# Block 0 of a fused eight-stage transformer kernel: the bf16 parts of the row maxima made on GpSimd, not on VectorE

## The chip, the cores and the metric

One core of a Trainium2 chip runs the whole program. The metric is the device time in microseconds of one execution, as the median of several runs. One execution is profiled, and its trace gives the start and duration of every instruction on every engine.

## The reference

The input is x of 16 batches x 56 tokens x 128 features, a conditioning vector per batch, and a context of 16 x 1500 x 128. Eight stages follow, each adding its result to x: four attention stages and four feed-forward ones. The change lies in the first, six layers of adaptive layer norm, self-attention with rotary embedding, cross-attention to the context and an MLP. Its attention is the usual one, with 16 heads of 8 features:

```python
def _attn(q, k, v, mask):
    scores = jnp.einsum('bqhd,bkhd->bhqk', q, k) / np.float32(np.sqrt(HD))
    scores = jnp.where(mask[:, None, None, :], jnp.float32(-jnp.inf), scores)
    w = jax.nn.softmax(scores, axis=-1)
    return jnp.einsum('bhqk,bkhd->bqhd', w, v)
```

In the cross-attention each of 16 batches has 56 queries and 1500 keys per head; over six layers these are 96 passes.

## The kernel before

The kernel computes the softmax's exponentials with keys on the partitions and queries along the columns, so the row maximum of a query can't be taken there. It is taken beforehand from a second set of score products with queries on the partitions, and is then fed into the first set of products as extra rows of the matmul: the maxima, negated, are split into three bf16 parts (high, middle, low) whose sum has nearly float32 precision, and the key side has rows of ones for them.

A pass is called a batch here, numbered 0 to 95 (16 a layer). Block 0 runs over slots s, each of 12 steps kt = 0 to 11. Every engine's program walks the same slots and steps in the order written in the code, and semaphores connect them. In slot s:

- `score_tensor` (L1528) makes the scores of batch s, a step's 125 keys at a time in two halves, ScalarE takes their exponentials (L2019), and `weigh_tensor` (L1554) multiplies them with the values one step later.
- `max_tensor` (L1542) makes the second set of products, two a step. Their maxima are taken on VectorE (L1898) out of two PSUM banks that alternate, into `row_max`, 112 queries x 8 head pairs x 3 thirds of the keys. Steps 0 to 9 finish batch s + 1, steps 10 and 11 begin batch s + 2.
- The keys of batches s + 2 and s + 3 are projected (L1568), rotated and split into bf16 parts by VectorE (L1778, L1779), GpSimd (L2039 to L2049) and ScalarE (L1924, L1928), and the sync engine's queue moves the parts into `key_stack` (L1443), the mask rows (L1451) and the query parts into `query_stack` (L1461). The values are projected by L1576.
- At step 10 VectorE makes the parts of batch s + 1 (`max_parts_vector`, L1742 to L1750): the minimum over the three thirds of the negated maxima, then four operations of 112 x 8 elements, each waiting for the one before. TensorE then turns them (L1605, the `("rows", s + 1)` entry). At step 11 VectorE copies the turned rows to the query stack (`rows_vector`, L1794), ahead of its two maxima of that step, and TensorE's first scores of batch s + 1 wait for that copy.

A phase is 8 slots. Beside the cross-attention of 8 batches it carries, for the other half of the tokens, the MLP, the norms (`norm_gpsimd`, L2073 to L2078, in two halves at two successive steps), the rotary projections (L1650) and the self-attention. In GpSimd's program a step runs `query_gpsimd`, `key_gpsimd`, the norm halves and then the block-diagonal queries (L2111).

Order of GpSimd's steps, as written:

```python
if 0 <= s + 2 < NS:
    self.query_gpsimd(e, s, kt)
self.key_gpsimd(e, s, kt)
```

Of the kernel before, what the change touches and what calls it, by code (L numbers as in the profile page):

```python
# [7 lines left out]
ALU, ACT, AX = mybir.AluOpType, mybir.ActivationFunctionType, mybir.AxisListType  # L8
# [18 lines left out]
PAIRS, F2 = H // 2, 2 * D // H  # L27
# [77 lines left out]
def of_batch(a, b):  # L105
    return a[:, b * S:(b + 1) * S]
# [6 lines left out]
def spread(cols, n):  # L113
    p, m = cols.shape
    return cols.unsqueeze(2).broadcast_to([p, m, n])
# [67 lines left out]
class Setup:  # L183
# [19 lines left out]
    def gpsimd(self, e):  # L203
        k = self.k
        e.memset(k.ident[:, :], 0.0)
        e.memset(k.eps_col, EPS)
        e.memset(k.mean_w, 1.0 / D)
        e.drain()
        e.affine_select(out=k.ident[:, :], in_=k.ident[:, :], compare_op=ALU.not_equal, fill=1.0,
                        base=0, pattern=[[-1, 128]], channel_multiplier=1)  # L210
        e.drain()
        e.tensor_copy(k.ident_b[:, :], k.ident[:, :])
        e.drain().then_inc(k.consts_ready.sem, 1)
        e.wait_ge(k.select_arrived.sem, k.select_arrived())
        e.tensor_copy(k.gate_select, k.gate_select32).then_inc(k.select_ready.sem, 1)
# [992 lines left out]
NS = NL * B  # L1208
# [20 lines left out]
class Block0:  # L1229
# [507 lines left out]

    def max_parts_vector(self, e, s):

        neg, m = self.neg, self.m_part[:, 1:1 + 3 * PAIRS].rearrange("q (p j) -> q p j", j=3)  # L1740
        e.wait_ge(self.max_read.sem, self.max_read(s, 3 * PAIRS - 1))
        e.tensor_reduce(neg, self.largest[:, :, :], AX.X, ALU.min).then_inc(self.negated.sem, 1)  # L1742
        e.wait_ge(self.negated.sem, self.negated(s, 0))
        e.tensor_copy(m[:, :, 0], neg).then_inc(self.negated.sem, 1)
        e.wait_ge(self.negated.sem, self.negated(s, 1))
        e.tensor_tensor(neg, neg, m[:, :, 0], ALU.subtract).then_inc(self.negated.sem, 1)
        e.wait_ge(self.negated.sem, self.negated(s, 2))
        e.tensor_copy(m[:, :, 1], neg).then_inc(self.negated.sem, 1)
        e.wait_ge(self.negated.sem, self.negated(s, 3))
        e.tensor_tensor(m[:, :, 2], neg, m[:, :, 1], ALU.subtract).then_inc(self.parts_ready.sem, 1)  # L1750
# [331 lines left out]
    def gpsimd(self, e):  # L2082
        side = self.side
        e.memset(self.src_mask, 0.0)
        e.drain()
        for ks in self.k_stack:
            e.memset(ks[ROWS:ROWS_ALL, :, :], 0.0)
        e.drain().then_inc(self.zeros_ready.sem, 1)
        for s in self.slots():
            for kt in range(KT):  # L2090
                if 12 * (s % BH) + kt == T_MASKS and s < 0:
                    e.wait_ge(self.tables_arrived.sem, self.tables_arrived())
                    e.tensor_scalar(self.src_mask[0:1, :], self.src_mask8, LOW, None, ALU.mult)
                    e.tensor_scalar(self.mask_rows, self.ctx_mask8, LOW, None, ALU.mult)
                    e.drain().then_inc(self.masks_ready.sem, 1)
                if 0 <= s + 2 < NS:
                    self.query_gpsimd(e, s, kt)
                self.key_gpsimd(e, s, kt)
                ph, t = s // BH, 12 * (s % BH) + kt
                for name, at in T_NORM.items():  # L2100
                    layer = MLP_OF(ph) if name == "mlp" else NEXT_OF(ph)
                    if layer is not None and t - at - 5 in range(2):
                        self.norm_gpsimd(e, name, ph, layer, t - at - 5)
                for i, a in enumerate(T_SELF(ph) if NEXT_OF(ph) is not None else ()):
                    if t == a - 1:
                        if i == 0:
                            e.wait_ge(self.roped.sem, self.roped(ph, 0))
                        if i >= 2:
                            e.wait_ge(side.filled, side.at("sc", ph, i - 2))
                        q = of_batch(self.q_rot, SIDE_OF(ph) * BH + i).unsqueeze(1).broadcast_to([128, H, S])  # L2110
                        e.tensor_tensor(self.qd[:, i % 2, :].rearrange("p (h q) -> p h q", h=H), q,  # L2111
                                        spread(self.block_diag, S), ALU.mult).then_inc(self.q_blocked.sem, 1)
# [1506 lines left out]
```

## Time and profile before

| | us |
|---|---|
| median of 3 runs | 6531.23 |
| lowest and highest run | 6515.23, 6531.41 |
| the profiled execution's time | 6515.7 |
| its span in the trace | 6513.8 |
| block 0's batches, from the first to the last making of parts | 187 to 3356 in the span |

A row of the timeline has the start in us from the span's start, the duration, the engine, the line of the kernel, the operation, the tiles written and read, their shapes and how many instructions are merged; in brackets stands the engine's idle time before it and who ended that. PE is TensorE, DVE VectorE, ACT ScalarE, POOL GpSimd and SPq the sync engine's queue of transfers.

### The profile page before, as it was taken

The numbers are of one execution on the slowest core, as the hardware profiler recorded it, in microseconds if no ns is written. First come the engines' busy times: TensorE is split into PE (matmuls) and PEld (weight loads), VectorE is DVE, ScalarE is ACT, GpSimd is POOL, SyncE is SP. The second block draws the span as 40 slices with busy tenths as digits, with TensorE's granted clock in tenths as the row PEclk, the third lists the DMA queues.
The fourth block names the chain that finished last, engine by engine and source line by source line (L and its number), as shares of the span: only waits on it lengthen the run. The fifth ranks groups of instructions, "written<-read, shape, count | busy, mean of one in ns | idle before, by whom it ended". The sixth has DMA issues, their size and how long they took to land. (4 is left out here: it accounts for less than half of the span.)

```text
span 6513.8 us, 141289 instructions
## 1 busy us (share of the span) xinstructions
PE 5993.6 (92%) x56229; PEld 4404.7 (68%) x56229; DVE 3931.8 (60%) x8724; ACT 3327.7 (51%) x6401; POOL 2244.3 (34%) x2180
## 2 busy tenths in 40 slices
PE   5899999998999989999989999999789999989998
PEld 4666666666666657666653778777557877856983
DVE  3777777777777777777765344444544444444552
ACT  1565656666566666666653334444334333333763
POOL 4555555555555555555520000000001111146430
PEclk7899999999999999999999899999889999998998
DMA  2665656656566565675750000000100000021000
GB/s 59 104 112 87 102 92 103 105 95 109 91 102 110 92 103 96 101 110 92 110 96 5 19 34 34 29 29 29 27 13 13 15 15 14 12 92 27 2 11 13
DMA packets 396488, 407.90 MB, mean 63 GB/s; under 512 B 125575, under 2 KB 372946, under 8 KB 393786
## 3 DMA queue, kind: packets, MB, share of 16 engines
q1 hardware_dynamic: 395834, 398.85, 34.6%
q8 instruction: 450, 7.37, 0.6%
q14 instruction: 204, 1.67, 0.1%
HBM read 158.00 MB, written 0.46 MB: 24 GB/s over the span
## 5 line engine op out<-in xcount | busy, mean ns | idle before, releaser
L1898 DVE TENSOR_REDUCE row_max<-psum 112x1 f32<-112x500 f32 x2304 | 1443.0, 669 | 271.5 <-PE psum L1542 266.9
L2019 ACT ACTIVATE weights<-psum 125x448 f32<-125x448 f32 x2304 | 1153.0, 545 | 715.5 <-PE psum L1528 700.4
L1528 PEld LDWEIGHTS psum<-query_stack,key_stack 121*125 121x125 bf16 x9216 | 832.3, 139 | 355.3 <-issue 153.8
L1542 PE MATMUL psum<-key_stack,query_stack 97*112 97x500 bf16 x2304 | 899.0, 391 | 110.4 <-DVE row_max L1898 87.2
L1528 PE MATMUL psum<-query_stack,key_stack 121*125 121x112 bf16 x9216 | 916.3, 222 | 72.7 <-ACT weights L2019 65.0
L2782 POOL TENSOR_TENSOR l_ctx_v<-l_ctx_v,l_ctx_w 125x512 f32<-125x512 f32 x48 | 61.0, 1270 | 2160.6 <-DVE l_ctx_v L2776 2160.6
L2309 DVE TENSOR_REDUCE l_stat<-psum 128x1 f32<-128x1500 f32 (+1 forms) x224 | 391.6, 1748 | 599.0 <-PE psum L2194 599.0
L2236 PE MATMUL psum<-l_ctx_v,l_turned 125*128 125x128 f32 x5376 | 699.5, 278 | 43.8 <-ACT l_w L2283 35.6
L2236 PEld LDWEIGHTS psum<-l_ctx_v,l_turned 125*128 125x128 f32 x5376 | 643.6, 191 | 64.7 <-issue 50.7
L1554 PE MATMUL psum<-weights,values 125*17 125x112 f32 x18432 | 674.6, 265 | 0.2 <-ACT weights L2019 0.2
L2266 ACT ACTIVATE l_turned<-psum 125x512 f32<-125x512 f32 x448 | 268.2, 599 | 670.9 <-PE psum L2218 670.9
L1554 PEld LDWEIGHTS psum<-weights,values 125*17 125x17 f32 x18432 | 377.6, 97 | 259.2 <-ACT weights L2019 137.5
L2039 POOL TENSOR_TENSOR key_temp<-key_temp,rope_sin 128x500 f32<-128x500 f32 x288 | 359.7, 1249 | 468.5 <-DVE key_temp L1778 468.5
L2049 POOL TENSOR_TENSOR key_parts<-key_temp,key_parts 128x500 bf16<-128x500 f32 x288 | 327.2, 1136 | 535.8 <-ACT key_parts L1928 535.8
L2046 POOL TENSOR_TENSOR key_temp<-key_temp,key_parts 128x500 f32<-128x500 f32 x288 | 327.7, 1138 | 351.8 <-ACT key_parts L1924 351.8
L2218 PE MATMUL psum<-ident,l_weights 128*125 128x128 f32 x2800 | 421.3, 274 | 7.0 <-ACT l_weights L2292 7.0
L1542 PEld LDWEIGHTS psum<-key_stack,query_stack 97*112 97x112 bf16 x2304 | 304.5, 132 | 154.5 <-issue 78.2
L2218 PEld LDWEIGHTS psum<-ident,l_weights 128*125 128x125 f32 x2800 | 369.0, 188 | 57.9 <-issue 39.0
L2292 ACT ACTIVATE l_weights<-psum,l_stat 128x1500 f32<-128x1500 f32 (+1 forms) x224 | 344.6, 1539 | 119.3 <-DVE l_stat L2309 118.5
L2043 POOL TENSOR_TENSOR key_temp<-key_temp 128x500 f32<-128x500 f32 x288 | 358.0, 1243 | 41.9 <-POOL key_temp L2039 0.9
L1576 PE MATMUL psum<-l_w_context,ctx_t 128*125 128x128 f32 x2304 | 342.5, 294 | 0.3 <-DVE key_temp L1779 0.3
L1568 PE MATMUL psum<-ctx_t,l_w_context 128*128 128x500 f32 x576 | 328.2, 653 | 2.4 <-ACT values L1945 2.4
(537 smaller groups left out, 10261.4 us busy)
## 6 DMA issues: line engine op xcount, KB each, us to landing
key_stack<-key_parts SPq DMA_DIRECT2D x1728, 125.0 KB, 4.5
ctx_t<-in_ctxT SPq DMA_DIRECT2D x96, 750.0 KB
l_ctx_v<-in_ctxV SPq DMA_DIRECT2D x32, 750.0 KB
query_stack<-query_parts SPq DMA_DIRECT2D x576, 28.0 KB, 3.6
l_ctx_t<-in_ctxT SPq DMA_DIRECT2D x16, 750.0 KB
slot_context<-in_ctxV SPq DMA_DIRECT2D x16, 750.0 KB
key_stack<-ctx_mask_rows SPq DMA_DIRECT2D x576, 3.9 KB
sm_w<-in_sm_w SPq DMA_DIRECT2D x3, 2048.0 KB
```

The lines of the kernel that those rows point to most:

```text
L1528: mm = e.matmul(self.k.psum[0:KN, h, (p % 4) * QC:(p % 4 + 1) * QC], ks[:, p, kt * KN:(kt + 1) * KN], q[:, p * QC:(p + 1) * QC])
L1542: e.matmul(self.k.psum[0:QC, 2 + n % 2, 0:500], q[0:ROWS_MAX, p * QC:(p + 1) * QC], ks[0:ROWS_MAX, p, c * 500:(c + 1) * 500]).then_inc(sel ...
L1554: mm = e.matmul(self.k.psum[32 * j:32 * j + 17, 5, g * QC:(g + 1) * QC], v[:, kt, p, :], w[:, p * QC:(p + 1) * QC], start=kt == 0 and g == ...
L1576: mm = e.matmul(side.bank(*key)[0:KN, i * 128:(i + 1) * 128], self.ctx_t[b % 2][:, t * KN:(t + 1) * KN], self.wk[b // B % 2][:, 1, :])
L1898: e.tensor_reduce(self.largest[:, i % PAIRS, i // PAIRS:i // PAIRS + 1], k.psum[0:QC, 2 + i % 2, 0:500], AX.X, ALU.max, negate=True).then_ ...
L2019: e.activation(half(self.p[kt % 2], h), self.k.psum[0:KN, h, 0:HALF], ACT.Exp).then_inc(self.exped.sem, 1)
L2039: e.tensor_tensor(tm[:, 1, :], tm[:, 1, :], self.sin[:, c * 500:(c + 1) * 500], ALU.mult).then_inc(self.key_turned_sin.sem, 1)
L2043: e.tensor_tensor(tm[:, 0, :], tm[:, 0, :], tm[:, 1, :], ALU.add).then_inc(self.key_rotated.sem, 1)
L2218: tr = e.transpose(bk[0:KN, t * 128:(t + 1) * 128], self.p[j % 2][:, c0:c0 + KN], k.ident[:, :])
L2236: mm = e.matmul(k.psum[:, 6, 0:128], pt[:, t, :], v[:, t, :], start=t == 0, stop=t == self.tiles - 1)
L2292: e.activation(self.p[i % 2][:, 0:self.width].rearrange("p (c n) -> p c n", c=self.n_s), k.psum[:, 0:self.n_s, 0:self.step], ACT.Exp, bias ...
L2309: e.tensor_reduce(self.stat[i % 4][:, 1:2], k.psum[:, 0:self.n_s, 0:self.step], AX.XY, ALU.max, negate=True).then_inc(self.max_ready.sem, 1)
```

## The change

Of `max_parts_vector` VectorE keeps the reduce over the thirds and the wait for its end, and gets a wait for the parts of the batch before, which read the same `neg_max` tile. The four operations that make the parts move to a new function `max_parts_gpsimd`, in which GpSimd waits for the reduce and for the turning of the batch before. It is called at step 10 of a slot, ahead of the query, key and norm work of that step. Semaphores count as before.

```diff
--- before.py
+++ after.py
@@ -1737,10 +1737,18 @@
 
     def max_parts_vector(self, e, s):
 
+        e.wait_ge(self.max_read.sem, self.max_read(s, 3 * PAIRS - 1))
+        if s > 0:
+            e.wait_ge(self.parts_ready.sem, self.parts_ready(s - 1))
+        e.tensor_reduce(self.neg, self.largest[:, :, :], AX.X, ALU.min).then_inc(self.negated.sem, 1)
+        e.wait_ge(self.negated.sem, self.negated(s, 0))
+
+    def max_parts_gpsimd(self, e, s):
+
         neg, m = self.neg, self.m_part[:, 1:1 + 3 * PAIRS].rearrange("q (p j) -> q p j", j=3)
-        e.wait_ge(self.max_read.sem, self.max_read(s, 3 * PAIRS - 1))
-        e.tensor_reduce(neg, self.largest[:, :, :], AX.X, ALU.min).then_inc(self.negated.sem, 1)
         e.wait_ge(self.negated.sem, self.negated(s, 0))
+        if s > 0:
+            e.wait_ge(self.side.filled, self.side.at("rows", s - 1))
         e.tensor_copy(m[:, :, 0], neg).then_inc(self.negated.sem, 1)
         e.wait_ge(self.negated.sem, self.negated(s, 1))
         e.tensor_tensor(neg, neg, m[:, :, 0], ALU.subtract).then_inc(self.negated.sem, 1)
@@ -2093,6 +2101,8 @@
                     e.tensor_scalar(self.src_mask[0:1, :], self.src_mask8, LOW, None, ALU.mult)
                     e.tensor_scalar(self.mask_rows, self.ctx_mask8, LOW, None, ALU.mult)
                     e.drain().then_inc(self.masks_ready.sem, 1)
+                if 0 <= s + 1 < NS and kt == 10:
+                    self.max_parts_gpsimd(e, s + 1)
                 if 0 <= s + 2 < NS:
                     self.query_gpsimd(e, s, kt)
                 self.key_gpsimd(e, s, kt)
```

## Rows read from the trace of the kernel before

**Rows 1.** The page, busy time, share of the span and instructions of each engine.

```profile
PE 5993.6 (92%) x56229; PEld 4404.7 (68%) x56229; DVE 3931.8 (60%) x8724; ACT 3327.7 (51%) x6401; POOL 2244.3 (34%) x2180
```

**Rows 2.** Windows: busy us (instructions) of each engine over block 0's batches.

```profile
187.00:3356.00 3169.00, 2959.58 (x37507) 2087.58 (x37507) 2419.20 (x5240) 1993.94 (x4096) 1706.79 (x1696) 0.98 0.63 101
```

**Rows 3.** Windows and tile view of neg_max_parts: its VectorE instructions, ns min/median/max.

```profile
187.00:3356.00 3169.00, 104.73 (x384) 0.98 0.63 101
...
L1744 DVE CAST neg_max_parts<-neg_max x96: 178/180/780, 188.1 to 3355.3; 112x8 bf16<-112x8 f32 x96
```

**Rows 4.** Groups by shape on GpSimd, whole span: busy us, mean ns, idle before.

```profile
L2061 POOL TENSOR_TENSOR query_block<-query_block,query_parts 128x112 f32<-128x112 f32 x96 | 38.5, 401 | 0.0
...
L215 POOL CAST gate_select<-gate_select_f 24x8 bf16<-24x8 f32 x1 | 0.2, 181 | 2.4 <-DMA gate_select_f<-in_gate_select 2.4
...
L3612 POOL MEMSET const-float32-1.0<- 128x1 f32 x1 | 0.1, 112 | 0.0
```

**Rows 5.** Waits in block 0's batches: us in total, times, longest.

```profile
PE psum L1650 <- POOL x_normed L2078: 14.8, 17, 0.9
...
PE psum L1605 <- DVE neg_max_parts L1750: 8.0, 12, 0.7
...
PE psum L1528 <- DVE query_stack L1794: 7.7, 11, 0.7
```

**Rows 6.** Timeline at batch 42 (place 2): start, duration, instruction, idle before.

```profile
1614.29 0.18 DVE L1742 TENSOR_REDUCE neg_max<-row_max 112x8 f32<-112x24 f32 x1
...
1614.53 0.56 POOL L2076 TENSOR_TENSOR x_normed<-x_normed,adaln_scale_shift 128x224 f32<-128x224 f32 x1
...
1615.17 0.57 POOL L2078 TENSOR_TENSOR x_normed<-x_normed,adaln_scale_shift 128x224 f32<-128x224 f32 x1
...
1615.70 1.13 POOL L2046 TENSOR_TENSOR key_temp<-key_temp,key_parts 128x500 f32<-128x500 f32 x1
...
1618.17 0.56 POOL L2078 TENSOR_TENSOR x_normed<-x_normed,adaln_scale_shift 128x224 f32<-128x224 f32 x1
...
1616.14 0.21 PE L1605 MATMUL psum<-ident_bf,neg_max_parts 112*128 112x112 bf16 x1
...
1618.79 1.02 PE L1650 MATMUL psum<-x_normed,l_w_attend 128*128 128x448 f32 x2 [0.87 <-POOL x_normed L2078]
```

**Rows 7.** Timeline at batch 45 (place 5), VectorE and TensorE.

```profile
1727.49 0.17 DVE L1742 TENSOR_REDUCE neg_max<-row_max 112x8 f32<-112x24 f32 x1
...
1729.46 0.21 PE L1605 MATMUL psum<-ident_bf,neg_max_parts 112*128 112x112 bf16 x1 [0.69 <-DVE neg_max_parts L1750]
```

**Rows 8.** Timeline at batch 47 (place 7) and batch 94.

```profile
1789.13 1.24 POOL L2043 TENSOR_TENSOR key_temp<-key_temp 128x500 f32<-128x500 f32 x1
...
1789.64 0.77 DVE L1744 CAST neg_max_parts<-neg_max 112x8 bf16<-112x8 f32 x1
...
1791.33 0.21 PE L1605 MATMUL psum<-ident_bf,neg_max_parts 112*128 112x112 bf16 x1
...
1794.56 0.58 PE L1554 MATMUL psum<-weights,values 125*17 125x112 f32 x16
...
3336.88 0.21 PE L1605 MATMUL psum<-ident_bf,neg_max_parts 112*128 112x112 bf16 x1
...
3339.45 0.58 PE L1554 MATMUL psum<-weights,values 125*17 125x112 f32 x16
```

**Rows 9.** Timeline behind batch 41 (place 1), the MLP projection and its input.

```profile
1583.20 0.56 POOL L2078 TENSOR_TENSOR x_normed<-x_normed,adaln_scale_shift 128x224 f32<-128x224 f32 x1
...
1583.97 1.67 PE L1633 MATMUL psum<-x_normed,l_w_mlp 128*128 128x448 f32 x4
```

**Rows 10.** Timeline around batch 47: TensorE's wait and the sync queue's transfers.

```profile
1789.06 0.42 PE L1542 MATMUL psum<-key_stack,query_stack 97*112 97x500 bf16 x1 [0.40 <-DMA query_stack<-query_parts]
...
1799.11 4.37 SPq L1451 DMA_DIRECT2D key_stack<-ctx_mask_rows  x6
...
1804.02 3.86 SPq L1443 DMA_DIRECT2D key_stack<-key_parts  x6
```

## The prediction

> **What bounds the kernel now.** I read the busy line of the page first: TensorE is busy 92% of the span, VectorE 60%, GpSimd 34% [rows 1]. The change touches block 0 only, so the next view is the sum over the stretch from the first to the last making of parts: 3169 us, TensorE 2960, VectorE 2419, GpSimd 1707 [rows 2]. TensorE is the spine: its own work fills 93%, and only what makes it wait, or spares it a wait, moves the end. The 209 us in which it is idle are short waits, and the list of waits says which touch this change: 12 waits of the transpose of the parts (L1605) for VectorE's last part (8.0 us), 17 waits of the rope projection (L1650) for GpSimd's normalisation (14.8 us), 11 waits of the first scores of a batch (L1528) for VectorE's copy of the rows (7.7 us) [rows 5]. After that I read the timeline at 96 batches. The pattern repeats every 8 batches, since a phase has 8 slots, so one timeline window stands for each place of it. I call them place 0 to 7: the number n of the batch whose parts are made, modulo 8.
>
> **What the change removes.** Four VectorE instructions per batch, 384 in all, 104.7 us busy [rows 3], so 1.09 us a batch of VectorE's queue, and four of its waits for itself. The shortest cast takes 0.18 us and the longest 0.78 [rows 3]; the long ones end as a GpSimd instruction ends: the cast runs from 1789.64 to 1790.41, GpSimd's sum from 1789.13 to 1790.37 [rows 8]. Before, a batch's chain from the reduce to the transpose thus costs between 1.0 and 1.8 us.
>
> **What it adds.** Four GpSimd instructions of 112 x 8, one behind the other, and two semaphore hops. No GpSimd instruction of block 0 is that narrow. The nearest row by shape is the setup's cast of 24 x 8, 0.18 us; the 128 x 112 subtraction takes 0.40 and the 128 x 500 one 1.13 [rows 4, 6], which is a line of 1.9 ns a column and gives 0.40 - 104 x 0.0019 = 0.20 at 8 columns. I take 0.19, bounded by 0.11 (a 128 x 1 memset) and 0.40 (the 112-wide subtraction) [rows 4]. Between dependent GpSimd instructions lie 0.08 us (1614.53 + 0.56 to 1615.17), and from GpSimd to TensorE 0.06 (1618.17 + 0.56 to 1618.79) [rows 6]; I take 0.08 from VectorE to GpSimd as well. The chain on GpSimd is 4 x 0.19 + 3 x 0.08 = 1.00 us.
>
> **Where GpSimd is not free: places 2 and 6.** In GpSimd's order the parts stand at slot step 10, behind the first half of a normalisation (step 9) and ahead of key work L2046 and the second half. At place 2 the reduce starts at 1614.29, but the first half's last instruction runs until 1615.74, L2046 begins at once at 1615.70, the second half ends at 1618.73, and TensorE, idle for 0.87 us, begins the projection at 1618.79 [rows 6]. The parts push all of that back by 1.00 us. The transpose, now at 1616.14, would come at 1616.76, but that 0.6 lies inside the longer wait behind it. So 1.00 us for each batch in which TensorE waits here: 17 of them by the waits [rows 5] (places 2 and 6 have 22 batches; in the other five TensorE comes over 1 us later). +17.0 us. The rope, its query and key work and the transfers that the sync engine issues behind L2049 hang on this projection and only move with it.
>
> **Where the stalled chain gets shorter: place 5.** The reduce starts at 1727.49 and takes 0.17, the transpose starts at 1729.46 after 0.69 us idle [rows 7]. GpSimd is free there, since the parts now stand ahead of L2046. New start: 1727.66 + 0.08 + 1.00 + 0.06 = 1728.80, so -0.66 us, 11 times (12 waits in all, the twelfth is the last batch). -7.3 us.
>
> **Where VectorE's relief reaches TensorE: places 7 and 0.** Here TensorE shows no wait behind the transpose, but its steps are stretched: from the transpose to the second weighing L1554 it takes 3.23 us (1791.33 to 1794.56), against 2.57 (3336.88 to 3339.45) for batch 94, where nothing holds VectorE up [rows 8]. VectorE's maxima free TensorE's two banks, and they queue behind the parts. With the parts gone the 0.66 comes back. The transpose: GpSimd is busy until 1790.37, parts until about 1791.33, transpose at 1791.39 instead of 1791.33, +0.06. The pattern of 3.2 to 3.3 us stands at 23 batches. In 14 of them (place 7 and batches 90 to 93) the next slot is short, and TensorE waits there for the landing of the query stack (0.40 us at 1789.06). The sync queue has little slack in such a slot: it ends the mask rows at 1803.48 and issues the keys at 1804.02 [rows 10], so those can gain 0.49 only. 14 x 0.49 + 9 x 0.60 = 12.3. -12.3 us.
>
> **Place 1.** TensorE waits 0.7 us for the rows' copy, 11 times [rows 5], since a reciprocal and the parts hold VectorE. That wait goes, but the next thing is late at once: the MLP projection starts at 1583.97 and its input is ready at 1583.76 + 0.06 [rows 9], untouched by VectorE. 0.15 x 11: -1.6 us. At places 3 and 4 the transpose comes well after the parts and waits for other work; they stay.
>
> Sum: 17.0 - 7.3 - 12.3 - 1.6 = -4.2 us. The profiled execution took 6515.7 us (span 6513.8 and 1.9 around it), so 6511.5; it lies 15.5 us under the median of the timed runs, 6531.2, and against that median I forecast **6527 us**: no change that can be told. A measurement of this kernel tells about 0.3% (20 us) from nothing. With the price of a part at its ends: at 0.11 us the terms are +11.6, -7.6, about -13 and -1.6, sum -11; at 0.40 the chain is 0.84 us longer and lies on the path at 17 + 11 + 23 = 51 batches, so -4.2 + 43 = +39.
>
> **A rule that speaks against the change.** The only cast of this width ran in 0.18 us on GpSimd, as on VectorE [rows 3, 4]. The Trainium skill (GPSIMD Engine Reference, "Engine selection") says that elementwise work belongs on VectorE and that GpSimd is about twice as slow with two inputs. What that would make of the time is the first rival.
>
> **Rivals.** *Narrow GpSimd instructions cost twice VectorE's* (slower). Price 0.35 us each: the chain is 1.64 us, 0.64 longer, at 51 batches: -4.2 + 32.6 = +28 us, 6560. It decides from about 0.31 us an instruction (0.47 us more a chain, times 51, is 24). For it: the 128 x 112 subtraction's 0.40; against it: the 24 x 8 cast and the line through the widths. The page's rule is this rival.
>
> *VectorE's relief stays with VectorE* (same): the stretched steps at places 7 and 0 come from something other than the maxima, ScalarE's exponentials for one. Then 12.3 goes and 23 x 0.06 comes: +17.0 - 7.3 + 1.4 - 0 to 1.6 = +10, 6541. Against it: at batch 94 the same ScalarE work stands and the steps are short.
>
> *The normalisation's delay is swallowed* (faster): TensorE or VectorE waits later at places 2 and 6 for something that does not move with the projection. Then -4.2 - 17.0 = -21, 6510. Against it: the 17 waits, and that the rope's chain starts from that projection.
>
> The change can hardly fail to do what it says: the four operations leave VectorE's program.
>
> **Numbers.** Forecast 0.50 (its own range 6515 to 6545), first rival 0.15, second 0.15, third 0.10, others 0.10, of which 0.06 slower and 0.04 faster. Faster by over 0.3%: 0.10 + 0.04 = 0.14; slower: 0.15 + 0.06 = 0.21; the rest, 0.65, within 0.3%. The range from 6505 to 6562 takes in the forecast and the centres of all three rivals, and leaves out the 0.40 us end.
>
> **What the changed profile would show.** Right: four GpSimd instructions near 0.2 us each, about 1 us a chain; L1650 waiting near 1.9 us for GpSimd at 17 batches; L1605 waiting 0.6 at places 2 and 6 and nearly nothing at place 5; second weighing 2.6 us behind the transpose at places 7 and 0; VectorE about 105 us less busy. Wrong: parts over 0.3 us each, waits of L1605 at places 3, 4, 7 or 0, the steps behind the transpose still 3.2 us, or larger waits for the query stack that take the gain back.

## The result, and the profile after

The changed kernel takes 6550.88 us (median of 17 runs, 6538.95 to 6568.87) where the kernel before takes 6527.7 (17 runs, 6514.43 to 6541.55): 1.0042 of its time, with an interval of 1.0034 to 1.0050. That is 23 us more. The forecast was 6527, no change that can be told. 6550.9 lies inside the whole range (6505 to 6562), but above the forecast's own (6515 to 6545) and past the 0.3% that "no change" allowed, and the mechanism behind it is one that the prediction did not name.

The parts did what the sum said they would. The page has VectorE 92 us less busy (105 were forecast: its other instructions took 12 us longer) and GpSimd 70 us more than in [rows 1]:

```profile
PE 6023.5 (92%) x56229; PEld 4420.8 (68%) x56229; DVE 3839.6 (59%) x8340; ACT 3323.8 (51%) x6401; POOL 2314.2 (35%) x2564
```

TensorE issues the same 56229 matmuls, and is recorded busy for 30 us longer. That is the first sign: the same work became slower. The stretch over block 0's batches is 3202 us long, against 3169 in [rows 2]; behind the engines' sums the row has the granted clock (0.97, before 0.98), the DMA share and GB/s.

```profile
187.00:3389.00 3202.00, 2989.30 (x37484) 2101.39 (x37485) 2326.33 (x4852) 1991.45 (x4094) 1775.12 (x2075) 0.97 0.63 99
```

The new GpSimd instructions, in the groups of instructions by shape (busy us, mean ns, idle before), answer to [rows 3, 4]:

```profile
L1758 POOL TENSOR_TENSOR neg_max_parts<-neg_max,neg_max_parts 112x8 bf16<-112x8 f32 x95 | 20.2, 213 | 7.7
L1754 POOL TENSOR_TENSOR neg_max<-neg_max,neg_max_parts 112x8 f32<-112x8 f32 x95 | 19.4, 204 | 7.7
L1756 POOL CAST neg_max_parts<-neg_max 112x8 bf16<-112x8 f32 x95 | 18.7, 197 | 6.1
L1752 POOL CAST neg_max_parts<-neg_max 112x8 bf16<-112x8 f32 x95 | 18.7, 197 | 48.5 <-DVE neg_max L1743 48.5
```

They cost 0.20 to 0.21 us each (0.19 was taken), so the chain is 1.03 us (1.00 was taken). The waits, in us in total, times and longest, answer to [rows 5]:

```profile
PE psum L1650 <- POOL x_normed L2086: 26.9, 22, 1.3
PE psum L1605 <- POOL neg_max_parts L1758: 10.9, 20, 0.6
```

The projection waits 12.1 us more than the 14.8 before. The wait for the copy of the rows, 7.7 us before, has no row left. The timeline at batch 42 shows place 2 as forecast: the transpose waits 0.55 us, and the second half of the normalisation ends at 1620.71.

```profile
1615.32 0.18 DVE L1743 TENSOR_REDUCE neg_max<-row_max 112x8 f32<-112x24 f32 x1
...
1616.19 0.56 POOL L2086 TENSOR_TENSOR x_normed<-x_normed,adaln_scale_shift 128x224 f32<-128x224 f32 x1
1616.69 0.20 POOL L1752 CAST neg_max_parts<-neg_max 112x8 bf16<-112x8 f32 x1
...
1617.52 0.21 POOL L1758 TENSOR_TENSOR neg_max_parts<-neg_max,neg_max_parts 112x8 bf16<-112x8 f32 x1
...
1617.88 0.21 PE L1605 MATMUL psum<-ident_bf,neg_max_parts 112*128 112x112 bf16 x1 [0.55 <-POOL neg_max_parts L1758]
1620.77 1.02 PE L1650 MATMUL psum<-x_normed,l_w_attend 128*128 128x448 f32 x2 [1.29 <-POOL x_normed L2086]
...
1632.01 0.64 PE L1542 MATMUL psum<-key_stack,query_stack 97*112 97x500 bf16 x1 [2.55 <-DVE row_max L1906]
```

The last of these rows is where the time goes. TensorE idles 2.55 us for VectorE's maxima, 14 us behind the transpose. The kernel before has that wait too, 2.56 us, and behind it the granted clock is at half (1.2 of 2.4 GHz). Before, it is back at full after 3.4 us. The wait, and the windows of TensorE (us, busy with instructions, granted clock, DMA share, GB/s), of the kernel before:

```profile
1630.05 0.39 PE L1542 MATMUL psum<-key_stack,query_stack 97*112 97x500 bf16 x1 [2.56 <-DVE row_max L1898]
...
1627.00:1630.40 3.40, 0.83 (x10) 0.99 0.02 4
1630.40:1633.80 3.40, 3.40 (x30) 0.51 0.02 5
1633.80:1637.20 3.40, 3.40 (x45) 1.00 0.00 0
```

The same place of the changed kernel:

```profile
1628.10:1631.50 3.40, 1.36 (x12) 1.00 0.24 24
1631.50:1634.90 3.40, 2.89 (x25) 0.50 0.02 5
1634.90:1638.30 3.40, 3.40 (x18) 0.50 0.00 0
1638.30:1641.80 3.50, 3.50 (x32) 0.50 0.00 0
1641.80:1645.20 3.40, 3.40 (x36) 0.51 0.16 41
1645.20:1648.60 3.40, 3.40 (x37) 1.00 1.11 137
```

It stays at half for 13.7 us, although TensorE is busy in all but half a microsecond of them; a product of 14 matmuls inside it (L1674) takes 3.08 us. This long form stands at places 2 of batches 42, 50, 58, 66 and 74 (there 17.1 us). Summed over the clock records from the first to the last minimum, TensorE has 109.2 us at half clock before (25 stretches) and 204.8 us after (38). By place the growth is 40.9 us behind place 2, 30.7 at place 5 and 20.4 at place 1: 92 of 95.6.

What a microsecond at half clock costs can be read at this same place. From the transpose of batch 42 to that of batch 43 the kernel before takes 41.16 us (1616.14 to 1657.30); the changed one takes 45.51:

```profile
1663.39 0.21 PE L1605 MATMUL psum<-ident_bf,neg_max_parts 112*128 112x112 bf16 x1
```

Of the 4.35 us more, 0.24 is the longer way to the projection (1617.88 to 1620.77, for 1616.14 to 1618.79 in [rows 6]); the other 4.1 us go with 13.7 - 3.4 = 10.3 us more at half clock, or 0.40 us for each. The Trainium skill (TensorE: Matmul & The Clock Gate, "Terms") puts that penalty at the time at the lower clock times one less the clock's share, which would be 0.5. The trace has 0.40 between the two kernels; inside the changed one, the same piece of place 2 takes 40.6 us with 3.4 at half clock (batch 34) and 45.5 with 13.7 (batch 42), which is 0.48. Over batches 8 to 87 of all fifteen traces of this document, each piece from transpose to transpose set against those of the same kernel and place, the slope is 0.43.

### The profile page after: what moved, and what is told of

Same layout as the page of the kernel before. It is cut to its first block and busy times, and to the rows that moved or that the text cites. A ratio compares the mean times of both kernels' runs of the same rounds, so it can differ in the third digit from the quotient of the medians.

```text
span 6549.1 us, 141575 instructions
## 1 busy us (share of the span) xinstructions
PE 6023.5 (92%) x56229; PEld 4420.8 (68%) x56229; DVE 3839.6 (59%) x8340; ACT 3323.8 (51%) x6401; POOL 2314.2 (35%) x2564
## 5 line engine op out<-in xcount | busy, mean ns | idle before, releaser
L1542 PE MATMUL psum<-key_stack,query_stack 97*112 97x500 bf16 x2304 | 903.4, 393 | 102.6 <-DVE row_max L1906 80.2
L1542 PEld LDWEIGHTS psum<-key_stack,query_stack 97*112 97x112 bf16 x2304 | 309.0, 134 | 133.2 <-issue 72.4
```

What stands on the lines that cost most here:

```text
L1542: e.matmul(self.k.psum[0:QC, 2 + n % 2, 0:500], q[0:ROWS_MAX, p * QC:(p + 1) * QC], ks[0:ROWS_MAX, p, c * 500:(c + 1) * 500]).then_inc(sel ...
```

## The account over all runs

One profile is one draw, and the kernel before spreads over 27 us. But every run's span and mean granted clock were recorded, so the time at half clock of a run is about 2 x (1 - clock) x span, for the whole program. The means over runs, each set against the kernel before on the same chip, make this table; "steps" is the difference in span less 0.40 of the difference at half clock.

```
run                              runs  ratio [95% interval]       span us   half clock us   steps us
e1_changed_again                   7   1.0040 [1.0026, 1.0054]    +25.4     +72             -3.4
e2_parts_back_at_2_6               9   0.9974 [0.9961, 0.9987]    -16.1     +13            -21.2
e3_parts_on_gpsimd_only_at_2_6     5   1.0064 [1.0049, 1.0080]    +43.4     +60            +19.5
e4_delay_alone_at_2_6              6   1.0063 [1.0048, 1.0079]    +42.7     +60            +18.6
e5_changed_fill_rope              11   0.9983 [0.9973, 0.9994]    -11.0     -43             +6.2
e6_before_fill_rope               12   0.9976 [0.9965, 0.9986]    -15.1     -58             +7.9
e7_changed_fill_both              11   0.9997 [0.9987, 1.0006]     -0.9     -63            +24.4
e8_split_fill_both                 9   0.9974 [0.9965, 0.9984]    -15.4     -85            +18.7
e9_split_fill_rope                 5   0.9951 [0.9937, 0.9964]    -33.5     -42            -16.9
e10_split_fill_three               5   0.9926 [0.9914, 0.9937]    -50.6     -80            -18.8
e11_before_again                  12   0.9998 [0.9988, 1.0008]     -0.9      -1             -0.3
e12_changed_fill_wait              5   1.0060 [1.0046, 1.0074]    +40.4     +39            +24.6
e13_before_busy_delay              5   1.0095 [1.0079, 1.0110]    +62.5     +39            +46.9
```

The kernel before has 625 to 653 us at half clock in these sets, most of it outside block 0's batches. The clock is recorded to 0.001, which is 13 us of half clock for one run and a few us for a mean. The traces give the steps a second time, as the stretch from first to last minimum less 0.40 of its own half clock, against the 3123.5 us of before: for e1 to e13 that is -8, -24, +14, +14, -3, +1, +22, +10, -24, -20, 0, +21 and +47 (and -3 for the first trace of the changed kernel). So a row of "steps" is good to some 5 us, and those of e5, e6, e8 and e9 only to 9. The price is the other doubt. Over 75 runs of the kernel before, span against half clock of the whole program has a slope of 0.28, not 0.40 (correlation 0.84). Half clock outside the batches, where TensorE waits for transfers too, may cost less, which was not tried. With 0.28 the first row's steps would be +5, and the clock still 20 of 25 us. The readings inside the stretch (0.40 to 0.48 above, 0.40 under e11) lie higher, so the table uses 0.40. Its first row is the finding: **the change's own steps are worth -3.4 us (between -8 and +5 with all doubts), where -4.2 was forecast, and 72 us more at half clock cost 0.40 x 72 = 29 us (20 at the lower price).**

## The experiments

**The changed kernel again, with no edit.** A second sample and a second trace of it.

> The changed kernel as it is, profiled a second time. Clock theory (the steps cost what the prediction says, -4 us, and the rest of the loss is TensorE granted half its clock for longer, 205 us of block 0's batches against 109 before, at about 0.4 us lost per us of half clock): ratio near 1.004, and if the time at half clock differs from 205 us in this profile, the last minimum (3389.4 us in the first profile) moves by 0.4 us for each us of it. Rival (the delay at places 2 and 6 costs far more than 1 us a batch through the queues behind it, whatever the clock): the last minimum stands at 3389 whatever the time at half clock.

6555.2 us. Its trace has 204.8 us at half clock between the first and last minimum, the very sum of the first one, but made otherwise: two stretches of 17.1 us behind place 2 in place of five long ones, and more short ones elsewhere, 41 in all. The stretch of block 0 is 3197.2 us, from 180.8 to 3378.0, against 3167.2 (187.9 to 3355.1) before and 3202.8 in the first trace. The last two have the same time at half clock and differ by 5.6 us, so the account is not exact.

**Each half of the change alone.** In the changed kernel the parts' maker is called by VectorE or by GpSimd, by place:

```
+ON_POOL = lambda n: n % 8 not in (2, 6)      # e2; e3 has: n % 8 in (2, 6)
...
+        if not ON_POOL(s):
+            self.make_parts(e, s)             # on VectorE
...
+        if ON_POOL(s):
+            self.make_parts(e, s)             # on GpSimd
```

> VectorE makes the parts at places 2 and 6, GpSimd at the other six. Clock theory: the steps alone give -21 us against before (-4.2 - 17.0), and to that come 0.4 us for each us at half clock above 109; so between -21 with the clock as before and about +10 with it as in the changed kernel. Rival (expensive delay at places 2 and 6): the whole loss goes, -21 to -24 us, ratio 0.9965, and the clock has no part. Second rival (the loss comes with the parts at the other places): still slower than before by 20 us or more.

> GpSimd makes the parts at places 2 and 6 only. Clock theory: the steps alone cost +17 us against before, plus 0.4 us for each us at half clock above 109. Rival (expensive delay): +45 to +55 us (the measured +34 of block 0 plus the 21 that the other places give back), with the time at half clock near 109. Second rival (other places at fault): within 5 us of before.

With the parts back on VectorE at places 2 and 6 the kernel takes 6511.23 us and beats the kernel before by 0.26%; with only places 2 and 6 on GpSimd it takes 6571.16, 0.64% slower. The forecast's terms are met: the other places give -21.2 us (7.3 + 12.3 + 1.6 = 21.2 were forecast), places 2 and 6 cost +19.5 (17.0 forecast). The sum of the two, -1.7, is the changed kernel's -3.4 within the error. And the clock is told apart with them: +13 us at half clock from the other places, +60 from places 2 and 6. So the loss is made where GpSimd is not free, and about half of its 43 us is not the wait but the clock (24 us at 0.40, 17 at 0.28).

**Only the delay, in the kernel before.** VectorE keeps the parts; GpSimd does one idle instruction of 448 columns (1.13 us) ahead of the second half of the normalisation, at places 2 and 6 alone.

```
+                if 0 <= s + 1 < NS and kt == 10 and (s + 1) % 8 in (2, 6):
+                    e.tensor_tensor(self.idle, self.cos[:, 0:448], self.sin[:, 0:448], ALU.mult)
```

> The kernel before, with one GpSimd multiplication of 128 x 448 into a tile that nobody reads (about 1.04 us by the line through the widths) at step 10 of places 2 and 6; VectorE makes all parts. Clock theory: like e3, +17 us of steps and the clock's share on top. Rival (expensive delay): like e3, +45 or more with the clock as before. If the transposes' own delay of 0.6 us mattered and not the projection's, this one would cost less than e3.

6572.53 us, the same as with the parts in its place, with the same +60 us at half clock and +18.6 us of steps. The projection's waits are 21.6 us longer than the 14.8 before:

```profile
PE psum L1651 <- POOL x_normed L2079: 36.4, 22, 2.0
```

So it does not matter what GpSimd does there. A delay of a microsecond of the projection is enough for both the steps and the clock.

**TensorE kept warm over the wait behind place 2.** The wait of 2.55 us for the maxima stands behind the projection of the self-attention's values (L1656). Four matmuls whose result nothing reads are put ahead of that product, in the changed kernel (e5) and in the kernel before (e6):

```
+            for i in range(4 if g == 1 and ph >= 0 else 0):
+                e.matmul(side.bank(*key)[:, 0:HALF], k.mean_w, self.cos[:, 0:HALF])
```

> The changed kernel with idle-filling work: four matmuls of 448 columns (mean_w times the cosine table, overwritten by the real product, so the output is the same) ahead of the last self-attention value product of each phase, just before TensorE's 2.55 us wait for VectorE in the slot behind place 2. They add some 1.7 us of TensorE work eleven times. Clock theory: the fall of the clock to half that follows this wait goes (about 92 of the 205 us at half clock), and with 0.4 us back for each, block 0's batches take some 35 us less than in the changed kernel, ratio to the kernel before 0.998 to 1.0. Rival (the time at half clock is not set off by TensorE's idling, or costs nothing): nothing is gained and the work costs up to 11 x 1.7 = 19 us, ratio 1.004 to 1.007.

> The kernel before with the same four matmuls. Clock theory: about 51 of its 109 us at half clock lie behind this wait and go, 15 to 20 us less, ratio 0.997; so the fill gives the changed kernel about twice what it gives this one, and the two kernels come nearer together. Rival: +0 to +19 us, and the same for both kernels.

Added work made both kernels faster, to 6521.12 and 6512.71 us. The expectations took the four for 1.7 us. They take 3.17, since an fp32 matmul of 448 columns is recorded as two instructions:

```profile
1622.36 3.17 PE L1656 MATMUL psum<-rope_cos,mean_weights 128*128 128x448 f32 x8
...
1626.75 0.38 PE L1542 MATMUL psum<-key_stack,query_stack 97*112 97x500 bf16 x1
```

The scores (L1542) no longer wait, and not one stretch at half clock is left behind place 2 in either trace. In the traces the half clock is 116.0 us with the change and 85.3 without. From e1 to e5 the changed kernel goes from +72 to -43 us at half clock, worth 0.40 x 115 = 46 us; by the table the fill costs 9.6 us of steps (the traces show almost none: their steps are -3 and +1), and the span falls by 36.4. With the clock nearly levelled, the change alone (e5 against e6) is worth +4.1 us of span, of which 0.40 x 15 = 6 is clock: -1.7, and in the two traces -4.3.

**The wait for ScalarE filled too.** TensorE also idles for ScalarE's exponentials, 2.4 us at places 5 and 1 and 1.2 at place 0. The first two waits get four matmuls and the third (the MLP's step) two, into the maxima's free bank, which the real products overwrite:

```
+                fill = {T_NORM["mlp"] + 3: 2, T_NORM["self"] + 3: 4, T_NORM["cross"] + 3: 4}.get(12 * (s % BH) + kt, 0)
+                if fill and 0 <= s < NS and self.max_at(s, kt):
+                    b, n = self.max_at(s, kt)
+                    e.wait_ge(self.max_read.sem, self.max_read(b, n) - 2)
+                    for i in range(fill):
+                        e.matmul(self.k.psum[:, 2 + n % 2, 0:HALF], self.k.mean_w, self.cos[:, 0:HALF])
```

e7 has it with the changed kernel, e8 with e2's; both have e5's fill too.

> e5, and more matmuls of the same kind ahead of the first scores of the step in which TensorE waits for ScalarE's square root and table loads (two behind the MLP norm's variance, four behind each of the two others), written into the maxima's bank and overwritten there. Clock theory: most of the time at half clock goes, from 205 us to under 40, so block 0's batches take about 3202.8 - 0.4 x 170 = 3135 us, ratio 0.990 to 0.993. Rival: the added matmuls, 11 x (1.7 + 0.9 + 1.7 + 1.7) = 66 us, mostly lie in waits, so near e5, or up to 50 us slower.

> e7's fills on e2's kernel (VectorE makes the parts at places 2 and 6). Clock theory: e2's steps (-21) without most of its 147 us at half clock: 3158.7 - 0.4 x 120 = about 3110 us for block 0's batches, 21 to 24 us under e7, ratio 0.987 to 0.990. Rival: like e2, 0.997, or slower.

This went too far: 6529.24 and 6515.96 us. The half clock fell by 63 and 85 us, but the steps grew to +24.4 and +18.7, since the fills are longer than the waits: 3.17 us for 2.4 and 1.67 for 1.2. The 33 waits sum to 65.1 us in e9's trace, and none is left in e8's:

```profile
PE psum L1529 <- ACT weights L2037: 65.1, 33, 2.4
```

The fills stand in 12 places of each kind, one more than the waits (they also run behind batches 0, 89 and 93, where TensorE does not idle so), and sum to 12 x (3.17 + 3.17 + 1.67) = 96 us. That is 31 us more than the waits, and it accounts for most of the 36 by which the table has e8's steps above e9's (33 by the traces).

**The split with e5's fill, and with fills of the right length.** e9 is e2 with e5's fill. e10 adds `fill = {T_NORM["self"] + 3: 3, T_NORM["cross"] + 3: 3}`, three matmuls (2.4 us) for the waits of 2.4 us at places 5 and 1, and none at place 0.

> e2 (VectorE makes the parts at places 2 and 6) with the four filling matmuls of e5 and e6 alone. By the sum that the runs so far bear out (block 0's batches = 3123.5 us + the steps' share + 0.4 us for each us at half clock): steps -21 to -24, time at half clock 147 - 24 = about 123 us, so about 3150 us, 17 us under the kernel before and 9 under e2; ratio 0.995 to 0.997. Rival (fill and split don't add up, since the falls move to other places): ratio 0.9975, as e2 and e6 each.

> e9 and three filling matmuls of 448 columns ahead of the scores behind the variance of the self and the cross norm (e8 had four there and two behind the MLP norm's). If e8's loss of about 25 us of steps against what its clock gives came from fills longer than the waits, this one gives half of it back or more: block 0's batches 3140 to 3150 us, ratio 0.995; if the falls only move on to the next wait, 0.997 as e8.

6505.23 and 6486.24 us. The last is the best version, 0.74% faster than the kernel before and, by the two ratios (0.9926 and 1.0042), 1.2% faster than the changed one. By the table it is -18.8 us of steps and -80 us at half clock (-32). Its minima run from 184.5 to 3316.7:

```profile
L1752 DVE TENSOR_REDUCE neg_max<-row_max x96: 119/178/179, 184.5 to 3316.7; 112x8 f32<-112x24 f32 x96
```

For e9 the account was put down ahead of the run, from the traces alone: the stretch should be 3123.5 + steps + 0.40 x half clock. About 3150 us with about 123 at half clock was expected; it measured 3149.1 with 122.9.

**The kernel before, traced again.** No edit.

> The kernel before, profiled a second time. The time at half clock in block 0's batches is not the same in each execution; whatever it is, the stretch from the first to the last minimum should be 3123.5 us plus 0.4 us for each us of it, within 5 us (109 us of it and 3167.2 us in the first profile). Rival (it is a fixed property of the kernel): 109 us again. Ratio 1.000.

Ratio 0.9998. Its trace caught an execution at the other end, 6547.3 us, and with it the account can be tried on two executions of one kernel: 150.2 us at half clock where the first trace has 109.2, and the stretch longer by 16.4 us (189.3 to 3372.9), which is 0.40 x 41.0 = 16.4.

```profile
L1742 DVE TENSOR_REDUCE neg_max<-row_max x96: 119/178/179, 189.3 to 3372.9; 112x8 f32<-112x24 f32 x96
```

The same program differs by that much from one execution to the next, and the profile on which the prediction rests (6515.7) was a light one.

**Is it the idle time in the longer wait, or the shift in time?** Matmuls that nothing reads are put ahead of the projection's wait for its input, so that TensorE is busy there, not idle: three in the changed kernel (e12), four in the kernel before (e13), where they are a delay with no idle time in it.

```
+            if n != 1 and ph >= 0:
+                e.wait_ge(side.emptied(*key), side.before(*key))
+                for i in range(3):            # e13: 4
+                    e.matmul(side.bank(*key)[:, 0:HALF], k.mean_w, self.cos[:, 0:HALF])
```

> The changed kernel with three matmuls of 448 columns (1.3 us, overwritten by the real product) ahead of TensorE's wait for the normalised values at places 2 and 6, the wait that the change makes longer. If the change's extra time at half clock comes from this wait's idleness, it falls from 205 us to the 109 to 150 us of the kernel before: block 0's batches 3121 + 0.4 x 130 = 3170 to 3185 us, ratio 1.000. If it comes from the shift in time that the delay brings to waits which the change does not touch (2.55 us for VectorE behind place 2, 2.35 us for ScalarE), it stays at 190 to 205 us, about 3200 us, ratio 1.004.

> The kernel before with four such matmuls at the same spot (1.7 us: they fill its 0.87 us wait and push the projection back by some 0.8 us with TensorE busy). If idleness there sets off the falls: steps +14 us, time at half clock no higher than in the kernel before (109 and 150 us in two profiles) or lower, 3181 to 3197 us, ratio 1.001 to 1.003. If the shift in time does it: time at half clock as in e3 and e4 (188 to 191 us), about 3213 us, ratio 1.006.

6569.69 and 6587.27 us. The fills were again longer than the expectations took them: 2.4 us against waits of 1.2 makes (2.4 - 1.2) x 22 = 26 us, and the steps went from -3.4 to +24.6; 22 fills of 3.1 us in place of 14.8 us of waits makes about 53, and +46.9 was measured. The half clock is +39 us in both, less than the +72 of the changed kernel and more than nothing. A delay in which TensorE is busy raises the time at half clock as well, so more idling in this wait is not the whole cause. How the two share it, these two times do not settle, since the fills also moved the schedule by more than the change does.

The traces tell more. Where no fill takes their place, two kinds of wait of 2.3 to 2.7 us come back in each phase, and in the fifteen traces a fall to half clock can be set against the end of the wait that it stands at (from 1.5 us before it to 2.2 us behind it; 92 of the 94 waits for the maxima stand at place 2):

```
                               waits  no fall  fall before the end      0 to 1.25 us behind  1.25 to 2 us behind
VectorE's maxima                 94      12    12: 13.7 or 17.1 (2: 6.8)   51: all 3.4       19: 10.2 or 13.7 (5: 3.4)
ScalarE, places 5 and 1         264      65    61: 6.8 (1: 3.4)           103: all 3.4       35: all 3.4
```

The length of a stretch goes with the moment at which the fall comes, in the same wait, in front of the same instructions. In the windows above, the clock falls some 0.5 us before the wait's end with the change (1631.5 for 1632.01) and 0.35 behind it in the kernel before (1630.4 for 1630.05): 13.7 us and 3.4. The falls before the end at place 2 are five and two in the two traces of the changed kernel, none and one in those of before. And how often a wait for ScalarE has a fall changes too: 18 of 44 in the two traces of before, 43 of 44 in those of the changed kernel, 35 of 44 in e3 and e4, and 15 of 22 in e13, where the delay has no idle time in it. It is 20 of 22 in e2 too, which has no delay at places 2 and 6; there it is the wait behind place 2 that has fewer, 4 of 11. These waits are as long in all of them, so the counts go with shifts of the schedule of either kind, and the delay is not their only cause. The extra time at half clock comes at waits that the change does not lengthen, by more falls and by other moments of them.

## Why the prediction was wrong

The failed step is "So 1.00 us for each batch in which TensorE waits here ... +17.0 us", and with it the sum: it took the cost of a delay to be the delay. The delay was there, near the size forecast (+19.5 in e3 by the table, +14 by its trace). On top of it came 60 us more at half clock, 24 us, and 29 us for the change as a whole (17 and 20 at the lower price). The prediction read the granted clock only as a mean (0.98 in [rows 2]) and never asked which waits it falls behind, though the wait of 2.56 us that starts those stretches was in the trace of before. None of the rivals had it.

- *The price of a part* (0.19 us): 0.197 to 0.213. The chain is 1.03 us for 1.00. VectorE's are 0.17 to 0.18, so GpSimd's cost 1.1 to 1.2 times as much, not twice. The rival of slow narrow instructions (0.35 each) fell, though its 6560 lies nearer to the result than the forecast: a right sign from a wrong reason.
- *Place 5*, -0.66 forecast: the reduce starts at 1733.57 and the transpose 1.41 us later, 1.97 in [rows 7], so -0.56.

```profile
1733.57 0.17 DVE L1743 TENSOR_REDUCE neg_max<-row_max 112x8 f32<-112x24 f32 x1
...
1734.98 0.21 PE L1605 MATMUL psum<-ident_bf,neg_max_parts 112*128 112x112 bf16 x1
```

- *Places 7 and 0*: the second weighing stood 3.23 us behind the transpose in [rows 8] and stands at 2.57 now, as forecast; the rival "the relief stays with VectorE" fell. The transpose comes 0.22 us later behind the reduce (2.07 for 1.85), not 0.06, mostly since GpSimd's last part reaches TensorE after 0.15. A short slot, from transpose to transpose, gains 0.48 (25.86 for 26.34), forecast 0.49.

```profile
1796.48 0.42 PE L1542 MATMUL psum<-key_stack,query_stack 97*112 97x500 bf16 x1 [0.41 <-DMA query_stack<-query_parts]
...
1796.55 1.25 POOL L2051 TENSOR_TENSOR key_temp<-key_temp 128x500 f32<-128x500 f32 x1
...
1798.56 0.21 POOL L1758 TENSOR_TENSOR neg_max_parts<-neg_max,neg_max_parts 112x8 bf16<-112x8 f32 x1
...
1798.92 0.21 PE L1605 MATMUL psum<-ident_bf,neg_max_parts 112*128 112x112 bf16 x1
...
1801.49 0.58 PE L1554 MATMUL psum<-weights,values 125*17 125x112 f32 x16
```

- *Place 1*: the second weighing comes 0.63 us earlier, and the MLP projection takes it back, as forecast. Places 3 and 4 stayed.
- *Places 2 and 6*: "near 1.9 us" for the projection's wait was wrong, 1.29 was measured, because the transpose ahead of it had already waited 0.55 of the same delay. All 22 batches wait, not 17; the steps, +19.5 by the table and +14 by the traces of e3 and e4, are too coarse to show what that adds to 17.0. "The normalisation's delay is swallowed" fell.

**What stays open.** Why more falls come, and at other moments of the waits, when the projection comes a microsecond later. The falls stand at waits that the change leaves alone (2.55 us for the maxima behind place 2, 2.4 us for ScalarE at places 5 and 1), and yet there are 38 in place of 25, and five recoveries take 13.7 us or more where 3.4 did before. That their length goes with the moment of the fall is shown by the table of waits above. One delay repeated in a schedule of 8 batches might bring its waits to another phase of whatever the chip watches; that is argued, not shown, and the two traces of each kernel differ too much to say how the growth divides between more falls and other moments. Shown is that the extra time at half clock comes with the delay alone (e4), whatever makes it, and that it is gone behind place 2 once TensorE is busy in the wait of 2.55 us (e5, e6).

## What to carry to other kernels

A delay on the tensor engine's path has two prices, its own length and what it does to the clock: before costing one, sum the time at the lower clock by place, find which waits it falls behind, and price it (0.40 us for each here, 0.28 to 0.48 by other readings). Move small work to a second engine only where that engine is free: the same four instructions gained 16 us in six places of the cycle (e2) and lost 43 in two (e3). Idle waits of 2 to 3 us on a busy tensor engine can be worth filling with matmuls that nothing reads; measure their length first. Three (2.4 us) in waits of 2.4 gained. Four (3.17 us) gained in a wait of 2.55 behind which all falls went, and lost in waits of 2.4, with more in a shorter wait and in three places without one (e8).

## What the runs showed of the hardware

- Four more matmuls in each of 11 places, 35 us of added work, make the kernel 15 us faster (e6), since the clock does not fall behind the wait.
- A TensorE that is busy 13.19 of 13.70 us stays at half clock throughout:

```profile
1631.50:1645.20 13.70, 13.19 (x99) 0.50 0.05 11
...
1908.00:1921.70 13.70, 13.14 (x99) 0.50 0.04 11
```

- Two executions of one kernel had 109 and 150 us at half clock in the same stretch. With the correlation of 0.84 over 75 runs, most of this kernel's spread goes with the clock.
- A fall to half clock within 1.25 us behind the end of a wait of 2.3 to 2.7 us lasted 3.4 us in all 154 cases of fifteen traces; one before the end of the wait lasted 6.8 us or longer in 72 of 73, up to 17.1.
- GpSimd's instructions of 8 columns cost 0.20 to 0.21 us, VectorE's 0.18; between dependent ones on GpSimd lie 0.08 us, and from the last of them to TensorE 0.15 (0.06 from the normalisation's last instruction, 1620.71 to 1620.77).
